# A token tower on one core: chunks of 512 tokens become chunks of 256, with activations doubled by parity and a new periodic list of steps for each engine

## The reference, cut to what matters

```python
h = w0[ids] @ w1 * (ids != 0) * 16          # w0: 8000 x 512, w1: 512 x 256
# block "attn", on x = layernorm(h)
n = layer_norm(x, ln1_g, ln1_b); s = token_shift(n)
k, v = (n*mk + s*(1-mk)) @ wk, (n*mv + s*(1-mv)) @ wv
r = sigmoid((n*mr + s*(1-mr)) @ wr)
x = x + (r * wkv_scan(k, v, time_decay, time_first)) @ wo
n = layer_norm(x, ln2_g, ln2_b); s = token_shift(n)
kk = relu((n*ck + s*(1-ck)) @ cwk) ** 2     # cwk: 256 x 1024
x = x + sigmoid((n*cr + s*(1-cr)) @ cwr) * (kk @ cwv)
h = h + x
# block "ffn", on x = layernorm(h); q() is FP4 in blocks of 16
a = silu(q(x) @ q(w_gate).T) * (q(x) @ q(w_up).T)   # 704 columns
h = h + q(a) @ q(w_down).T
```

## Time and profile before

| what | value |
| --- | --- |
| time, median of 3 runs (lowest, highest) | 788.66 us (787.74, 792.24) |
| time of the profiled execution | 790.58 us |
| span of the profiled execution | 788.8 us |
| PE busy | 698.7 us, 89% of the span |
| DVE busy | 600.1 us, 76% |
| ACT busy | 511.7 us, 65% |
| POOL busy | 147.8 us, 19% |

### The profile page before, as it was taken

How to read it: one execution, slowest core, us unless ns; L and a number is a source line. 1 busy time by engine, 2 the same in 40 slices (tenths; PEclk the granted TensorE clock), 3 DMA queues, 4 the chain that set the end, 5 groups by cost and what they waited for, 6 DMA issues and landing times.

```text
span 788.8 us, 9882 instructions
## 1 busy us (share of the span) xinstructions
PE 698.7 (89%) x3311; PEld 566.1 (72%) x3311; DVE 600.1 (76%) x1023; ACT 511.7 (65%) x889; POOL 147.8 (19%) x220
## 2 busy tenths in 40 slices
PE   3353699699999999999999999999999999799686
PEld 2231576589688977888688958897789778688574
DVE  0797835987788888788788778888878888863763
ACT  1267488668874887389757886588748974761221
POOL 2042230433023300421022302330131003100000
PEclk9677799899999999999999999999999999899988
DMA  5800000000010000100010001000100000000000
GB/s 133 230 27 25 3 27 0 28 1 27 1 41 14 26 3 14 41 1 27 14 34 8 28 14 27 15 28 0 35 20 1 1 14 15 1 0 14 15 0 27
DMA packets 11956, 19.34 MB, mean 25 GB/s; under 512 B 972, under 2 KB 9346, under 8 KB 11906
## 3 DMA queue, kind: packets, MB, share of 16 engines
q1 hardware_dynamic: 9302, 10.31, 4.5%
q0 software_dynamic: 2560, 8.39, 3.7%
q10 hardware_dynamic: 44, 0.01, 0.0%
HBM read 14.51 MB, written 4.19 MB: 24 GB/s over the span
## 4 chain that ended last, share of the span: by engine, by line
PE 69%; DVE 15%; ACT 7%; issue 6%; DMA 2%; POOL 0%; SPq 0%; DVEq 0%; ACTq 0%; POOLq 0%
PE psB L546 17%; PE psB L573 11%; PE psC L642 11%; PE psC L615 11%; PE psA L537 9%; PE psA L509 3%; PE psC L629 3%; ACT mix L796 2%; DMA kkT<-L_ffn_w_gate 2%; DVE top L352 1%; DVE mix L1082 1%; PE psB L519 1%; PE psA L519 1%; DVE top L949 1%; ACT take L790 1%
## 5 line engine op out<-in xcount | busy, mean ns | idle before, releaser
L546 PE MATMUL psB<-cwv_s,kkT 128*128 128x256 f32 x512 | 113.2, 379 | 0.0
L546 PEld LDWEIGHTS psB<-cwv_s,kkT 128*128 128x128 f32 x512 | 96.6, 190 | 16.0 <-issue 3.7
L642 PE MATMUL psC<-downT,hqT 128*128 128x256 f32 (+1 forms) x384 | 97.0, 398 | 0.0
L429 POOL DMA_INDIRECT rows<-L_tok_w,ids_now x32 | 45.7, 1427 | 266.7 <-PE psA L497 255.1
L615 PE MATMUL psC<-up_hi,xq_hi 128*128 128x352 f32 x256 | 88.3, 345 | 7.4 <-DVE xq_lo L1194 6.8
L642 PEld LDWEIGHTS psC<-downT,hqT 128*128 128x128 f32 (+1 forms) x384 | 70.2, 193 | 26.7 <-issue 19.0
L537 PE MATMUL psA<-mix,kvr_s 128*128 128x512 f32 x192 | 86.8, 596 | 1.5 <-DVE mix L963 1.3
L615 PE MATMUL psC<-up_hi,xq_lo 128*128 128x352 f32 x256 | 84.0, 328 | 0.0
L615 PE MATMUL psC<-up_lo,xq_hi 128*128 128x352 f32 x256 | 83.9, 328 | 0.0
L537 PEld LDWEIGHTS psA<-mix,kvr_s 128*128 128x128 f32 x192 | 35.8, 190 | 41.1 <-issue 38.4
L963 DVE SCALAR_TENSOR_TENSOR mix<-hT,rest,mix 128x512 f32<-128x512 f32 x80 | 54.3, 747 | 10.3 <-ACT mix L744 10.3
(11 more groups left out here) (163 smaller groups left out, 1435.6 us busy)
## 6 DMA issues: line engine op xcount, KB each, us to landing
out<-h SPq DMA_DIRECT2D x16, 256.0 KB, 2.1
mix<-L_attn_cwk SPq DMA_DIRECT2D x1, 1024.0 KB, 15.7
cwv_s<-L_attn_cwv SPq DMA_DIRECT2D x1, 1024.0 KB, 16.0
kkT<-L_ffn_w_gate SPq DMA_DIRECT2D x1, 704.0 KB
kkT<-L_ffn_w_up SPq DMA_DIRECT2D x1, 704.0 KB
hqT<-L_ffn_w_down SPq DMA_DIRECT2D x1, 704.0 KB, 17.9
w_s<-L_tok_w SPq DMA_DIRECT2D x1, 512.0 KB, 4.0
rows<-L_tok_w,ids_now POOLq DMA_INDIRECT x32, 4.1
```

What stands on the lines that cost most here:

```text
L429: pool.indirect_dma_start(rows[:, q, :], None, tok_w0, bass.IndirectOffsetOnAxis(ap=ids_now[:, s, t:t + 1], axis=0)).then_inc(rows_in[q], 16)
L546: mm = nc.tensor.matmul(psB[:, B.slot(name), q * D:(q + 1) * D], lhsT[:, k, (2 * j + q) * P:(2 * j + q + 1) * P], weight[:, k, :], start=( ...
L642: mm = nc.tensor.matmul(psC[:, C.slot(name), 0, q * D:(q + 1) * D], hqT[0:n, q, k, :], downT[0:n, k, :], start=(k == 0), stop=(k == KI - 1))
```

## The change: what it does

A chunk becomes one sequence of 256 tokens: 16 chunks of two tiles each. `h0`, `y`, `hT`, `mix`, `rT`, `hT2`, `rows` and the coefficients get two buffers, used by the chunk's parity, and the residual `h1` four; `kT`, `vT`, `top`, `keep`, `take` and `takev` stay single, and `e_new`, `numer`, `norm` and `x1` get storage of their own. `Jobs` numbers the PSUM jobs over the whole program, in the order in which they come. The five lists of `ORDER` are new, with lags from -5 to 5.

Operations that took one half of the features for 512 tokens now take both halves for 256 tokens, and so keep 512 columns: relus and squares of the keys, exponentials, the scan's products, k, v, r. Those with a parameter per partition or a recurrence (mixes, norms' affine step, `rise` and `fall`, the first scan) become operations of 256 columns, as many in a round as before. The copies of the turned product (L890 to L892) become one of 768 columns. The raw weights of gate and up are loaded as rows of 128 partitions, 11 x 128 values each, and quantised in halves of 704 columns; a half goes through its first four stages (`w_scale`) and then its last three (`w_round`). SP waits for the rows of chunk 1, where it waited for those of chunk 0 alone, before it starts the loads of gate, up, cwk, down, wo, cwr and cwv. One ACT table set that holds both logarithm and exponential is loaded by hand ahead of `a_wkv1` and `a_wkv3`.

```diff
-CHUNK = 512
-CHUNKS = TOKENS // CHUNK
-NT = TOKENS // P
+CHUNK = T
+CHUNKS = SEQS
+NT = SEQS * T // P
 TILES = CHUNK // P
...
-AHEAD = 2
+KEPT = 4
...
-    "pool": [("gather1", 1), ("c_coef0", 3), ("c_coef1", 3), ("b_sum", 2), ("b_coef", 2), ("a_coef", 1),
-        ("gather0", 0)],
-    "sp": [("c_down1", 3), ("c_down0", 2)],
...
+    "pool": [("b_sum", 1), ("b_coef", 1), ("c_coef", 2), ("a_coef", -1), ("gather", -3)],
+    "sp": [("c_down", 0)],
...
+A_JOBS = [("xt0", "act", 0), ("xt1", "act", 0), ("e", "act", 0), ("n", "act", 0), ("k", "act", 0), ("v", "act", 0),
+          ("r", "act", 0)]
+B_JOBS = [("o", "dve", 0), ("t", "act", 0), ("kk0", "act", 0), ("kk1", "act", 0), ("kk2", "act", 0), ("kk3", "act", 0),
+          ("rr", "act", 0), ("cv", "dve", 0)]
+C_JOBS = [("q", "dve", 0), ("g0", "act", 0), ("u0", "dve", 0), ("hq1", "act", 1), ("d", "dve", 1), ("g1", "act", 0),
+          ("u1", "dve", 0), ("hq0", "act", 0)]
...
+RELOAD = ["rise0"] + ["log"] * any(step in between("a_wkv1", "a_wkv3") for step in ("a_r", "b_gate", "c_up0", "c_up1"))
...
+        rows = sb("rows", [P, UNROLL, TILES, E])
+        rowsT = sb("rowsT", [P, TILES, KE, P])
+        h0 = sb("h0", [P, UNROLL, TILES, D])
+        mv_a = sb("mv_a", [P, UNROLL, TILES, 2])
+        sc_a = sb("sc_a", [P, UNROLL, 10, TILES])
+        norm = sb("norm", [P, TILES, D])
+        y = sb("y", [P, UNROLL, TILES, D])
+        hT = sb("hT", [P, UNROLL, H, ROW])
+        mix = sb("mix", [P, UNROLL, 3, H, T])
+        kT = sb("kT", [P, H, T])
+        vT = sb("vT", [P, H, T])
+        rT = sb("rT", [P, UNROLL, H, T])
+        top = sb("top", [P, H, ROW])
+        keep = sb("keep", [P, H, ROW])
+        take = sb("take", [P, H, ROW])
+        takev = sb("takev", [P, H, ROW])
+        e_new = sb("e_new", [P, H, T])
+        numer = sb("numer", [P, H, T])
...
+        raw_gate = flat(kkT)[:, 0:GJ * P].rearrange("p (j d) -> p j d", d=P)
+        raw_up = sb("raw_up", [P, GJ, P])[:]
+        raw_down = hqT[:].rearrange("p s k n -> p s (k n)")
+        raw = (raw_gate, raw_up)
...
+            for q in range(TILES):
+                sp.wait_ge(rows_in[1][q], 16)
             for k, w in enumerate((w_gate, w_up)):
-                sp.dma_start(raw_up[:, k * GJ:(k + 1) * GJ, :], w.rearrange("(j p) d -> p j d", p=GP)).then_inc(s_raw[k], 16)
-            sp.dma_start(raw_down, w_down.rearrange("(h p) n -> p h n", p=P)).then_inc(s_raw[2], 16)
+                sp.dma_start(raw[k], w.rearrange("n (h d) -> (n h) d", h=H).rearrange("(j p) d -> p j d", p=P)).then_inc(s_raw[k], 16)
             sp.dma_start(raw_key, cwk.rearrange("(k p) d -> p k d", p=P)).then_inc(s_raw[3], 16)
+            sp.dma_start(raw_down[:, :, 0:INTER], w_down.rearrange("(h p) n -> p h n", p=P)).then_inc(s_raw[2], 16)
...
+                    name, kk = f"kk{j}", flat(kkT[:, 2 * j:2 * j + 2])
+                    B.wait_full(act, ch.back(1), "cv")
+                    B.wait_full(act, ch, name)
+                    nc.scalar.activation(kk, psB[:, B.slot(ch, name)], ACT.Relu).then_inc(b_act, 1)
+                    B.wait_emptied(act, ch, name)
+                    nc.scalar.activation(kk, kk, ACT.Square).then_inc(kk_done.sem, 1)
...
+                if names[0] in RELOAD:
+                    nc.scalar.preload_act_table_set(LOG_EXP)
...
+                    tt(take[:, :, now], kT[:], top[:, :, past], ALU.subtract)
+                    for d in range(H):
+                        did("gain")
+                        nc.vector.tensor_scalar(e_new[:, d], take[:, d, now], col("time_first", d), BEYOND, ALU.add, ALU.min
+                                                ).then_inc(wkv.sem, 1)
```

More of the change, by code:

```diff
@@ L174 @@
-EXPS = [f"{step}{d}" for step in ("rise", "fall", "keep", "take", "new", "log", "inv") for d in range(H)]
-QUANT = 7
+        if ch.exists():
+            self.emptied_by(engine, self.place[name, ch.base])
+A_JOBS = [("xt0", "act", 0), ("xt1", "act", 0), ("e", "act", 0), ("n", "act", 0), ("k", "act", 0), ("v", "act", 0),
+          ("r", "act", 0)]
+B_JOBS = [("o", "dve", 0), ("t", "act", 0), ("kk0", "act", 0), ("kk1", "act", 0), ("kk2", "act", 0), ("kk3", "act", 0),
+          ("rr", "act", 0), ("cv", "dve", 0)]
@@ L345, in wide @@
                 return t.unsqueeze(2).to_broadcast([p, nb, BLOCK])
-            for stage in range(QUANT):
+            for stage in stages:
                 for k, (data, w, big, scale, p, nb) in enumerate(parts):
@@ new lines, in step, with emb @@
+                    name = f"xt{t}"
+                    A.wait_full(act, ch, name)
+                    nc.scalar.copy(flat(rowsT[:, t]), psA[:, A.slot(ch, name)]).then_inc(a_act, 1)
+                return step
+            def emb(ch):
+                at(act, ids_cut, ch, 2)
+                at(act, b_sum, ch.back(2), 1)
+                A.wait_full(act, ch, "e")
+                for t in range(TILES):
+                    a = nc.scalar.activation(h0[:, ch.parity, t, :], psA[:, A.slot(ch, "e"), t * D:(t + 1) * D], ACT.Identity,
+                                             scale=mask_now[:, ch.parity, t:t + 1])
+                a.then_inc(a_act, 1)
@@ L778, in exponentials @@
                         "keep": (k, k, ACT.Exp, -1.0, 0.0),
                         "take": (t, t, ACT.Exp, -1.0, 0.0),
-                        "new": (n, n, ACT.Exp, 1.0, 0.0),
+                        "new": (e_new[:], e_new[:], ACT.Exp, 1.0, 0.0),
                         "log": (t, k, ACT.Ln, 1.0, 0.0),
                         "inv": (t, t, ACT.Exp, -1.0, 0.0),
-                    }[step]
-                    made = {"rise": "gain", "fall": "now", "new": "now", "log": "denom"}
-                    before = {"fall": "rise", "keep": "rise", "take": "fall", "inv": "log"}
@@ new lines, in gate_b, with norm_c, cols_c @@
+                B.wait_full(act, ch, "rr")
+                nc.scalar.activation(flat(rr), psB[:, B.slot(ch, "rr")], ACT.Sigmoid).then_inc(b_act, 1)
+            def norm_c(ch):
+                at(act, c_coef, ch, 4)
+                if ch.base == 0:
+                    act.wait_ge(s_wq, QUANT * WPARTS * 3)
+                C.wait_full(act, ch.back(1), "q")
+                normed(ch, normc, mine(ch), sc_c[:, ch.parity], 1, 3, c_norm)
+            def cols_c(ch):
+                C.wait_full(act, ch.back(1), "u1")
+                C.wait_full(act, ch, "q")
+                nc.scalar.copy(flat(xq_hi), psC[:, C.slot(ch, "q"), 0]).then_inc(c_high.sem, 1)
@@ L888, in turned @@
[L888 to L892 removed]
+                    k, n = divmod(j, WPARTS)
+                    act.wait_ge(s_wq, QUANT * WPARTS * k + SCALED * (n + 1))
+                    nc.scalar.activation(square_w[n], halves(k, n), ACT.Square, scale=SPREAD).then_inc(s_sq, 1)
@@ L975, in expd @@
                     at(dve, wkv_exp, ch, EXPS.index(name) + 1)
-                def both(where, fn):
-                    if part == where:
-                        for d in range(H):
-                            fn(d).then_inc(wkv.sem, 1)
-                now, before = slice(1, ROW), slice(0, T)
                 def stt(out, in0, scalar, in1, op0, op1):
-                    return nc.vector.scalar_tensor_tensor(out=out, in0=in0, scalar=scalar, in1=in1, op0=op0, op1=op1)
+                    nc.vector.scalar_tensor_tensor(out=out, in0=in0, scalar=scalar, in1=in1, op0=op0, op1=op1).then_inc(wkv.sem, 1)
@@ L1034, in wkv_a @@
-                both(2, lambda d: nc.vector.tensor_tensor_scan(long(take, d), long(keep, d), long(take, d), 0.0, ALU.mult, ALU.add))
-                def f_newv(d):
-                    expd(f"new{d}")
-                    A.wait_full(dve, ch, "v1")
-                    return tt(numer[:, d], e_new[:, d], vT[:, d], ALU.mult)
-                both(2, f_newv)
-                def f_numer(d):
-                    after(f"newv{d}")
-                    return tt(numer[:, d], numer[:, d], takev[:, d, :, before], ALU.add)
```

965 lines of the change are left out of this document (426 added, 539 removed), and 21 rows, old and new, of the table ORDER.

## The result

The changed kernel takes 834.98 us (median of 4 runs, 832.97 to 836.22) against 788.2 us of the kernel before (4 runs): a ratio of 1.0575, 95% interval 1.0551 to 1.06 (this and the ratios below are the record's, worked out over single runs; the two medians alone give 1.059). It is slower, as forecast, but by 5.75% and not by 2.2%, and lies 5 us above the range of 772 to 830. The profiled execution has a span of 832.7 us. One of the 11 executions of experiment 5 took 983.62 us at a mean granted clock of 0.716; the ratios are of undisturbed runs, and its trace is not read.

What follows compares the result with a forecast made beforehand. The prediction took PE to bound the old rounds and an ACT-DVE loop of 43.7 us the new ones. Its terms, 96.5 + 34 + 41 + 524 + 37 + 74, made a span of 806.5, forecast 806 us, range 772 to 830.

Steps and rivals of the forecast that it cites:

- full rounds: Middle chunks: a loop of ACT's and DVE's lists takes 43.7 us, above PE's 42.2; 12 rounds make 524.
- prices of 256-column operations: Short operations on ACT and DVE: 0.42 us for one on ACT, 0.41 for a DVE mix.
- Rounds and drain: From keys 0 to the end: 34 + 41 + 524 + 37 + 74 us, added to 96.5 for a span of 806.5.
- the drain: From keys 15 to the end: 57 us for the last chunk plus 17, so 74; bounds 62 and 85.
- the shortened round: From keys 14 to keys 15, with steps missing from the lists: 37 us, against 43.7 for a full round.
- the ffn of chunk 14: In the drain: this work and the last scans, ahead on DVE, add 17 us.
- Keys 1 to 2: Early round in which DVE's list has only a part of the ffn steps: 41 us.
- The fill: From the start to the keys of chunk 0: 96.5 us against 109.31 before; bounds 90 and 105.
- The last leg: End of the fill, from the scan's last part at 84 to the keys of chunk 0 at 96.5 us.
- a range of 12 us to each side of the sum: The forecast's own range around 806 us, from 794 to 818.
- A: Rival, whole kernel: loop shorter than PE's 42.2 us, PE without gaps from keys 0 on; 777 us, faster; chance 0.24.
- The case in between: Rival: full rounds at 42.2 us, first ones and drain as worked; 789 us, no change; chance 0.14.

Runs made afterwards that it cites:

- experiment 5: Changed kernel with the logarithm and exponential table set loaded once a round for the scan, four loads a round instead of six: 789.84 us, ratio 0.9997.
- Experiments 1 to 3: Each against the changed kernel: load ahead of the relus removed, 805.98 us; that load moved outside the loop, 807.96; one key matmul pass left out, 832.44.
- experiment 1: Changed kernel without the hand-made table load ahead of the scan's relus: 805.98 us, ratio 1.0204 to the kernel before.
- experiment 4: Changed kernel with the last chunk's quantisation of normc ahead of the second ffn tile of the chunk before: 824.79 us, ratio 1.0449.
- experiment 6: As experiment 5, with ACT's y moved from ahead of the scan's logarithm to behind the gate's sigmoid: 789.63 us, ratio 1.0003.
- experiments 5 to 7: Changed kernel with one table load for the scan, 789.84 us; that plus y moved on ACT, 789.63; one load plus one key pass less, 788.57.

## Why the prediction was wrong in size

**Sign and mechanism of the full rounds: right.** Full rounds are set by the loop of ACT's list from `key_hi` to the square and DVE's from there to the mixes, 43.75 us for 43.7. Experiments 1 to 3 show it: a load taken out of the loop shortens the round by its own length, the same load outside the loop does not lengthen it, and PE's work doesn't matter. The prices of 256-column operations nearly hold: four mixes on DVE take 1.67 us (forecast 4 x 0.41), six take 2.75 (2.45).

**The step that failed: "Rounds and drain", the terms outside the full rounds.** They are 21 of the 26 us that the sum is short. The largest are the drain (74 forecast, 84.8 measured) and the shortened round ahead of it (37, 42.4). The forecast saw that the ffn of chunk 14 is ahead on DVE and gave it 17 us; that term was nearly right. What it had too small are the legs ahead of and behind that wait, as the chain of waits of the changed kernel shows:

```profile
764.46 0.70 DVE rr L1023
...
796.04 6.94 PE psC L615 x24
...
803.08 0.90 DVE hq L1046
...
804.03 5.45 PE psC L640 x24
809.47 3.86 PE psC L615 x24
...
813.42 0.90 DVE hq L1046
...
820.57 1.54 PE psC L630 x6
```

| leg of the drain | forecast us | measured us |
| --- | --- | --- |
| keys, gate, values (from 747.93 to 764.46) | 13 | 16.5 |
| sum, statistics, norm, and the ffn of chunk 14 (to 788.43) | 6 + 17 | 24.0 |
| quantisation, turn and halves (to 796.04) | 5 + 2 | 7.6 |
| gate and up with silu of the first tile (to 803.08) | 6 | 7.0 |
| two products with their quantisations (to 820.57) | 14 | 17.5 |
| turn, copy, down, sum and store (to 832.7) | 2.5 + 6 + 3 | 12.1 |

In the first leg PE's third group of keys waits 1.17 us, at 752.72, for a relu that stands on ACT's list behind a square of chunk 13's ffn, which waits for DVE, and gate and values alone take 8.65 us of PE. In the fifth, DVE's second product waits 2.66 us for PE, where the c_down of chunk 14 (804.03) stands ahead of the second tile's gate and up. In the fourth, the same 24 matmuls take 6.94 us that take 3.86 at 809.47, with a granted clock of 0.50 from 788.4 to 800 us (experiment 4 has the row up to 796). So the sum went along the last chunk's own chain and left out other steps of the lists and the clock. How the 10.8 us divide among these causes is read from one trace; no experiment takes them apart. Experiment 4 shows that another order of the last turn wins 10 us, which is not the same as what the sum lacked.

The shortened round 14 to 15 was taken to lose 7 us with its missing steps; it lost 1.3, since most of the loop's steps were still there. That only the loop counts, and not how much work a round holds, was the argument for the full rounds and should have been used for this one. Keys 1 to 2 (43.9 us, as long as a full round, with part of the ffn only) point the same way; the clock in the first rounds is a second cause there (experiment 1).

**The fill.** 99.2 for 96.5. Gate landed at 20.5, not 24.7, and the end of the scan was met exactly (84.0) all the same, which is luck: the steps from there on took 4.2 us longer than forecast. The last leg, 15.1 us where I had 12.5, was under-counted because the k product of chunk 1 on PE (89.75 to 93.55) and its scan's start on DVE (from 94.26) stand ahead of the first chunk's transposes and mixes.

**The range.** The drain lay within its own bounds, 62 to 85, at their very end. All six terms were too small at once. As I read it, they share a cause: each but the full rounds' was a sum along one chain that left out other steps of the lists, so their errors don't cancel, and a range of 12 us to each side of the sum was too narrow.

**The rivals.** A's price was wrong: in experiment 6, where PE's list sets the full rounds, the time is 789.6 and not 777, although a round of PE is 41.25 and not 42.2. Keys 0 come at 98.1 there, and PE has 650.8 us of work behind them, near A's 656, but it stands for 39.6 us behind them where A had 25. The case in between, 789, has the time of experiments 5 to 7, but by rounds of 41.25 in place of 42.2.

## What to carry to other kernels

Smaller chunks are worth the idle time of the busiest engine that they save, not the length of fill and drain: here that was 2 us in the fill, and each round's fixed costs (table loads, short operations) came twice as often. In lists that are worked in order, look for the loop through two or three lists, and count what stands in it; here a table load of 1.28 us inside the loop cost 1.25 in every full round, and outside it nothing in the round, until another loop or an engine's own list takes over. Go through the first and last turns list by list too: a periodic order that is good in the middle lets ready work wait there, and a different order for the last turn was worth 10 us.
